# Decoder block, last two stages: routing of four batches and the small expert's second layer placed among the last causal heads

## What is computed

```python
xf = _rms(x, n2_w).reshape(-1, C)
logits = jnp.nan_to_num(xf @ gate_w.T)
probs = softmax(logits); topv, topi = top_k(probs, 2)
topv = topv / (topv.sum(-1, keepdims=True) + 1e-08)
wts = zeros((N, E)).at[arange(N)[:, None], topi].add(topv)
o0 = _gelu(xf @ e0_up.T) @ e0_down.T
o1 = silu(xf @ e1_w1.T) * (xf @ e1_w2.T) @ e1_down.T
o2 = _gelu(_gelu(_gelu(xf @ e2_l1.T) @ e2_l2.T) @ e2_l3.T) @ e2_l4.T
o3 = _gelu(_gelu(xf @ e3_down.T) @ e3_up.T) @ e3_out.T
moe = wts[:, 0:1]*o0 + wts[:, 1:2]*o1 + wts[:, 2:3]*o2 + wts[:, 3:4]*o3
return x + moe        # first 64 channels of moe are zero; a layernorm follows
```

## Time and profile before

| what | value |
|---|---|
| three runs | 1126.34, 1134.78, 1134.48 us (median 1134.48) |
| profiled execution, its own time | 1130.39 us |
| its span, first to last instruction | 1128.6 us |
| mean granted PE clock | 0.928 of full speed |

### The profile page before, as it was taken

One profiled execution on the slowest core, in us unless ns is written; L12 is line 12 of the kernel. 1 busy time (PEld: TensorE's weight loads), 2 busy tenths in 40 slices (PEclk: granted clock), 3 DMA queues, 4 the chain that ended last, 5 costly groups with the idle time before them and its releaser, 6 DMA issues.

```text
span 1128.6 us, 22127 instructions
## 1 busy us (share of the span) xinstructions
PE 971.2 (86%) x8864; PEld 702.0 (62%) x8864; DVE 679.3 (60%) x1584; ACT 587.8 (52%) x1382; POOL 289.5 (26%) x297
## 2 busy tenths in 40 slices
PE   7997879987879998999898788888888888978995
PEld 4664556665458875666566566666566666646754
DVE  3346544664949955666565577766767666649204
ACT  4632555553438865454554345555456464666441
POOL 3421332100230007111121131222122132355443
PEclk9997878979889998999998889999999899988998
DMA  9350543500769978432262333304304104000001
GB/s 308 113 91 21 128 101 73 123 12 1 237 198 325 323 255 258 156 129 90 82 192 82 87 114 110 110 29 134 97 29 138 28 1 164 6 1 1 1 1 33
DMA packets 66678, 123.71 MB, mean 110 GB/s; under 512 B 11632, under 2 KB 41968, under 8 KB 62496
## 3 DMA queue, kind: packets, MB, share of 16 engines
q1 hardware_dynamic: 64528, 117.48, 34.1%
q0 software_dynamic: 2048, 4.82, 1.4%
HBM read 86.30 MB, written 35.92 MB: 108 GB/s over the span
## 4 chain that ended last, share of the span: by engine, by line
PE 53%; DVE 24%; ACT 11%; DMA 5%; issue 4%; POOL 2%; SPq 1%; DVEq 0%; ACTq 0%; POOLq 0%
PE psum L413 36%; ACT s_p L2803 3%; DVE s_p L2845 3%; DVE s_max L2834 2%; PE psum L2762 2%; PE psum L1410 2%; PE psum L2773 2%; DVE s_pT L2826 1%; DMA raw_wd<-in_wd 1%; PE psum L568 1%; PE psum L2236 1%; DVE junk L1930 1%; DVE s_max L687 1%; PE psum L2946 1%; PE psum L2754 1%
## 5 line engine op out<-in xcount | busy, mean ns | idle before, releaser
L2803 ACT ACTIVATE s_p<-psum,s_max 112x375 f32<-112x375 f32 x128 | 72.2, 569 | 98.8 <-DVE s_max L2834 98.8
L734 POOL TENSOR_TENSOR rstd<-meanvar,minus_half 112x1 f32<-112x1 f32 x40 | 25.7, 643 | 244.7 <-DVE meanvar L679 176.0
L687 DVE TENSOR_REDUCE s_max<-psum 112x2 f32<-112x750 f32 x64 | 59.4, 935 | 36.6 <-PE psum L568 35.8
L2762 PE MATMUL psum<-ident,s_p 112*125 112x112 f32 x384 | 63.1, 298 | 7.6 <-ACT s_p L2803 3.2
L2834 DVE TENSOR_REDUCE s_max<-psum 112x1 f32<-112x375 f32 x128 | 63.7, 540 | 2.2 <-PE psum L2754 2.0
L2754 PE MATMUL psum<-s_k,s_q 64*112 64x375 f16 x384 | 47.6, 354 | 20.2 <-ACT s_p L2803 8.2
L413 PE MATMUL psum<-Wv,ctx 128*125 128x512 f16 x240 | 60.6, 404 | 3.4 <-issue 2.6
L2762 PEld LDWEIGHTS psum<-ident,s_p 112*125 112x125 f32 x384 | 51.8, 200 | 17.5 <-DVE s_max L2834 5.2
L413 PE MATMUL psum<-ctx,Wk 128*128 128x375 f16 x320 | 61.7, 328 | 0.0
L3200 POOL TENSOR_TENSOR rs<-ms,minus_half 112x32 f32<-112x32 f32 x8 | 43.5, 5438 | 69.2 <-DVE ms L3128 69.2
L628 ACT ACTIVATE s_k<-psum 128x375 f16<-128x375 f32 x64 | 31.2, 491 | 52.2 <-PE psum L413 51.8
(11 more groups left out here) (402 smaller groups left out, 2481.4 us busy)
## 6 DMA issues: line engine op xcount, KB each, us to landing
keys<-s_k SPq DMA_DIRECT2D x64, 187.5 KB, 2.3
s_k<-keys SPq DMA_DIRECT2D x8, 1500.0 KB, 7.6
values<-s_v SPq DMA_DIRECT2D x48, 224.0 KB
s_v<-values SPq DMA_DIRECT2D x16, 672.0 KB
raw_wg<-in_wg SPq DMA_DIRECT2D x8, 1024.0 KB, 6.7
raw_wu<-in_wu SPq DMA_DIRECT2D x8, 1024.0 KB, 6.9
raw_wd<-in_wd SPq DMA_DIRECT2D x8, 1024.0 KB, 7.9
s_kd<-k_halves SPq DMA_DIRECT2D x48, 93.8 KB, 3.8
```

The costliest lines, as they stand in the source:

```text
L687: VE.tensor_reduce(s1_max[b % 2][:, 2 * p:2 * p + 2], rings["s1"][unit][0:N, :, 0:S], X, ALU.max, negate=True).then_inc(*V.up("max1", n))
L2762: ins = TE.transpose(rings["t4"][unit][0:SCH, c * N:(c + 1) * N], p[:, c * SCH:(c + 1) * SCH], ident[0:N, 0:N])
L2803: SC.activation(rings["p4"][2 * n + j], rings["s4"][(n, j)][0:N, 0:S], ACT.Exp, bias=s4_max[b % 2][:, h:h + 1], accum_out=s4_sum[b % 2][:, ...
```

## The change

1. The routing's arrays move to a region of their own (`route_m`), and each step works on one half (4 batches). Half 0 is routed in the causal heads' stage: stream `s5_first_route` waits for `gate5` of batch 3, then places a copy of the router's products (`tp6`), the steps and the exponential. Half 1 is routed in the last stage. `gate5` of batches 4 and 5 wait for the copy.
2. The filler's order: `gate5` 0 to 3 first, then the 14 products with e3_down ahead of e0_up, then four units `ly5`, which are e3_up for half 0 with Gelu, copy and subtraction, and then `gate5` 4 and 5. The Gelus of `la` follow the same new order and wait for the exponential of half 0.
3. In the last stage the second layer of e3 for half 0 is gone, and the sums come by halves: experts 0 and 1 half 0, e3_up half 1, expert 3 half 0, e2_l1 half 0, experts 0 and 1 half 1, e2_l1 half 1, expert 3 half 1. The weight splits follow: e3_out now comes ahead of e2_l1.

```diff
-    AHEAD = [(name, f) for name in ("e0_up", "e3_down", "e1_w1", "e1_w2")
+    AHEAD = [(name, f) for name in ("e3_down", "e0_up", "e1_w1", "e1_w2")
...
+    step("ly5", "T ly, A gelu, A lh, G ll", "misc5", "A gelu", 1150)
+    step("tp6", "V +2, V tp6")
+    step("r6", "V r6")
+    step("r6x8", "V +3, V r6")
+    step("exp6", "A exp6")
...
     def s5_ahead():
         yield from until(("out", 4, B - 1), ("xfT5e", 3), ("split5p", FIRST[3], KC - 1))
+        for b in range(4):
+            yield [("gate5", b)]
         for i, at in enumerate(AHEAD):
             yield from until_banks(1)
             yield [("aheadV" if i % 2 else "aheadA", *at)]
-            if 4 <= i < 8:
-                yield [("gate5", i - 4)]
+        for f in range(HT):
+            yield from until(("la", "e3_down", 0, KC - 1), ("la", "e0_up", 0, f), ("split5", "e3_up"))
+            yield from until_banks(1)
+            if f == 0:
+                rings["hidden"].take(("e3_up", 0), (T, ("ax", 3, 0, 3)))
+            yield [("ly5", "e3_up", 0, f)]
         for b in (4, 5):
             yield from until(("xfT5e", b))
             yield [("gate5", b)]
 
+    def s5_first_route():
+        yield from until(("gate5", 3))
+        yield [("tp6", 0)]
+        yield from route_until_exp(0)
+        yield [("exp6", 0)]
+        yield from route_behind_exp(0)
+
+    def route_until_exp(hf):
+        for n in range(5):
+            yield [("r6", hf, n)]
+
+    def route_behind_exp(hf):
+        for n in range(5, 22):
+            place(("r6x8" if n in (8, 9) else "r6", hf, n))
+            if n % 2:
+                yield None
+
     def s5_first_gelu():
-        yield from until(("s5e", B - 1, 3))
+        yield from until(("s5e", B - 1, 3), ("exp6", 0))
...
         elif what == "gate5":
             pe.wait_ge(A["oT4", B - 1, 1])
+            if b >= 4:
+                pe.wait_ge(V["tp6", 0])
             gate_product(b, T.up("gate5", b))
...
+        elif what == "ly5":
+            name, hf, f = at
+            raw_, dst = raw_rows(name, hf, f), rings["hidden"][name, hf]
+            act.wait_ge(T["ly", *at], G["ll", "e0_up", 0, f])
+            SC.activation(raw_, ring[unit][:, 0:HALF], ACT.Gelu,
+                          scale=1 / WSCALE).then_inc(*A.up("gelu", *at))
+            act.wait_ge(A["gelu", *at])
+            SC.activation(dst[:, 0, f, :], raw_, ACT.Copy).then_inc(*A.up("lh", *at))
...
     def s6_add(e, hf):
-        yield from until(("r6", 21), ("split5", ("e0_down", "e1_down", "e2_l4", "e3_out")[e]))
+        yield from until(("r6", hf, 21), ("split5", ("e0_down", "e1_down", "e2_l4", "e3_out")[e]))
...
         yield from s6_layer("e3_down", 1)
-        yield from s6_layer("e3_up", 0)
-        for e in range(2):
-            for hf in range(2):
-                yield from s6_add(e, hf)
+        yield from s6_add(0, 0)
+        yield from s6_add(1, 0)
         yield from s6_layer("e3_up", 1)
-        for hf in range(2):
-            yield from s6_layer("e2_l1", hf)
-            yield from s6_add(3, hf)
+        yield from s6_add(3, 0)
+        yield from s6_layer("e2_l1", 0)
+        yield from s6_add(0, 1)
+        yield from s6_add(1, 1)
+        yield from s6_layer("e2_l1", 1)
+        yield from s6_add(3, 1)
...
-                (w16_w, "e2_l1", ("ly", "e3_down", 1, 1)), (w16_w, "e3_out", ("ax", 0, 0, 0)),
-                (w16_w, "e2_l2", ("ax", 0, 0, 3)), (w16_w, "e2_l3", ("ax", 0, 1, 3)),
-                (w16_w, "e2_l4", ("ax", 1, 0, 3))):
+                (w16_w, "e3_out", ("ly", "e3_down", 1, 1)), (w16_w, "e2_l1", ("ax", 0, 0, 3)),
+                (w16_w, "e2_l2", ("ax", 1, 0, 3)), (w16_w, "e2_l3", ("ax", 3, 0, 3)),
+                (w16_w, "e2_l4", ("ax", 0, 1, 3))):
```

More of the change, by code:

```diff
@@ L2734, in build @@
           follow(s5_out, range(1, B, 2)),
-          s5_first_weights(), s5_first_gelu(), filler=ahead_units)
+          s5_first_weights(), s5_first_route(), s5_first_gelu(), filler=ahead_units)
     for units in ahead_units:
-        for unit in units:
+        for unit in units or ():
             place(unit)
@@ L3026, in gpsimd_gelu_low, with take_logits, scalar_route @@
                          ALU.subtract).then_inc(*G.up("ll", name, hf, f))
+    def take_logits(hf):
+        here = slice(4 * hf, 4 * hf + 4)
+        VE.tensor_copy(tp5[:, here], psum[0:N, GATE_BANK, 4 * hf * E1:(4 * hf + 4) * E1].rearrange(
+            "p (b e) -> p b e", e=E1)).then_inc(*V.up("tp6", hf))
+    def scalar_route(hf):
+        here = slice(4 * hf, 4 * hf + 4)
+        act.wait_ge(V["r6", hf, 4])
+        SC.activation(tp5[:, here], lg5[:, here], ACT.Exp).then_inc(*A.up("exp6", hf))
@@ new lines, in vector_route @@
+    def vector_route(what, hf, n):
+        if n:
+            dve.wait_ge(A["exp6", hf] if n == 5 else V["r6", hf, n - 1])
+        else:
+            dve.wait_ge(V["tp6", hf])
+        if what == "r6":
+            route(hf, n).then_inc(*V.up("r6", hf, n))
+            return
+        for b in range(4 * hf, 4 * hf + 4):
+            ins = VE.max(top5[:, b, :], pr5[:, b, :]) if n == 8 else \
+                VE.max_index(top5_i[:, b, :], top5[:, b, :], pr5[:, b, :])
+            ins.then_inc(*(V.up("r6", hf, n) if b % 4 == 3 else V.up()))
@@ new lines, in route, with wide4 @@
+    def route(hf, n):
+        here = slice(4 * hf, 4 * hf + 4)
+        mx, den, ts = (sm5[:, i, here] for i in range(3))
+        ok5_, tp5_, lg5_, cl5_, wt5_, pr5_, top5_ = (
+            t[:, here] for t in (ok5, tp5, lg5, cl5, wt5, pr5, top5))
+        def wide4(t):
+            return t.unsqueeze(2).to_broadcast([N, 4, E1])
+        if n == 0:
+            return VE.tensor_tensor(ok5_, tp5_, tp5_, ALU.is_equal)
+        if n == 1:
+            return VE.tensor_scalar(lg5_, tp5_, FMAX, -FMAX, ALU.min, ALU.max)
+        if n == 2:
+            return VE.copy_predicated(cl5_, ok5_, lg5_)
+        if n == 3:
+            return VE.tensor_reduce(mx, cl5_, X, ALU.max)
+        if n == 4:
+            return VE.tensor_tensor(lg5_, cl5_, wide4(mx), ALU.subtract)
+        if n == 5:
+            return VE.tensor_reduce(den, tp5_, X, ALU.add)
+        if n == 6:
+            return VE.reciprocal(den, den)
+        if n == 7:
+            return VE.tensor_tensor(pr5_[:, :, 0:E1], tp5_, wide4(den), ALU.mult)
+        if n == 10:
+            return VE.tensor_tensor(ts, top5_[:, :, 0], top5_[:, :, 1], ALU.add)
+        if n == 11:
+            return VE.tensor_scalar(ts, ts, 1e-8, WSCALE, ALU.add, ALU.mult)
+        if n == 12:
+            return VE.reciprocal(ts, ts)
+        if n == 21:
+            return VE.tensor_tensor(wt5_, wt5_, tp5_, ALU.add)
+        k, m = divmod(n - 13, 4)
+        dst = (wt5_, tp5_)[k]
+        if m == 0:
+            return VE.tensor_copy(ek5[:, k, here], top5_i[:, here, k])
+        if m == 1:
+            return VE.tensor_tensor(dst, iota8[:, 0:E1].unsqueeze(1).to_broadcast([N, 4, E1]),
+                                    wide4(ek5[:, k, here]), ALU.is_equal)
+        if m == 2:
+            return VE.tensor_tensor(sm5[:, 3, here], top5_[:, :, k], ts, ALU.mult)
+        return VE.tensor_tensor(dst, dst, wide4(sm5[:, 3, here]), ALU.mult)
@@ L3213, in gpsimd_s5 @@
                              ALU.subtract).then_inc(*G.up("xf16", b))
-        elif what == "la":
+        elif what in ("la", "ly5"):
             gpsimd_gelu_low(*at)
@@ L3309, in s6_route @@
     def s6_route():
-        yield [("gate6",)]
-        for n in range(5):
-            yield [("r6", n)]
-        yield from until(("exp6",))
-        for n in range(5, 22):
-            place(("r6x8" if n in (8, 9) else "r6", n))
-            if n % 2:
-                yield None
+        yield [("gate6", 1)]
+        yield from route_until_exp(1)
+        yield from until(("exp6", 1))
+        yield from route_behind_exp(1)
     def s6_split():
@@ L3394, in scalar_s6 @@
             elif what == "exp6":
-                act.wait_ge(V["r6", 4])
-                SC.activation(tp5[:], lg5[:], ACT.Exp).then_inc(*A.up("exp6"))
+                scalar_route(*at)
             elif what == "ly":
@@ L3416, in vector_s6 @@
         fence(dve, 5)
-        mx, den, ts = sm5[:, 0, :], sm5[:, 1, :], sm5[:, 2, :]
         def vector_gated_high(hf, f, raw_):
```

116 lines of the change are left out of this document (42 added, 74 removed).

## The result

The changed kernel takes 1145.95 us (median of 20 runs, 1134.08 to 1155.07), the kernel before 1129.52 us (20 runs, 1116.24 to 1138.74). The ratio is 1.0148, with a 95% interval of 1.0120 to 1.0177: slower by 1.5%, clear of the noise, and outside the range that was given (1123 to 1139 us).

What follows compares the result with a forecast made beforehand. It took PE's wait for DVE's first add of sums as the bound: +4.3 +0.3 −3.8 = +0.8 us on 1130.39 makes 1131.2, plus 1.1 for the runs' mean gives 1132.3 us, range 1123 to 1139.

Steps and rivals of the forecast that it cites:

- What bounds the end: Last stage: the end is fixed by when PE may pass its wait for DVE's first add of sums.
- Part 3: Last stage, from its first matmul to the first add: less routing and fewer POOL subtractions bring the add 3.8 us sooner.
- The clock behind the wait: Last stage: the clock's dip around the wait costs 2.3 us before and after; change 0, bounds −1.4 and +1.
- Part 1: Before the last stage: four early second-layer products load ACT ahead of the last batch's squares; stage starts 4.3 us later.
- Part 2: Causal heads: early routing of batches 0 to 3, about 6 us on DVE, mostly covered; +0.3 us, bounds −0.7 and +3.
- A: Rival, chance 0.22: ACT's idle time before the last stage hides the moved layer, stage only 1.5 us later; 1129 us.
- B: Rival, chance 0.08: in the last stage the wait and both clock dips vanish, products fill idle time; −12.7, 1119.8 us.
- D: Rival, chance 0.10: in the last stage second-half routing stays slow, first add 1.5 us sooner instead of 3.8; 1134.6 us.
- C: Rival, chance 0.13: in the heads early routing collides with POOL's power and delays the maxima, +6.4 us; 1138 us.
- the routing's short operations: Sign of being right: in the causal heads, routing operations of 0.2 us on DVE around 960 us.
- the wait for the first add: Sign of being right: in the last stage PE still waits near 5 us, ending near 1036.5 us.
- the 312 matmuls behind it: Sign of being right: after PE's wait in the last stage, 312 matmuls run unbroken before the second deep layer.

Runs made afterwards that it cites:

- e0_up: Not a run: the code's name for expert 0's early products, which the change places behind the small expert's first layer; no time of its own.
- e3_other_rows: Changed kernel, with the early second layer's Gelu writing into rows read long before; 1146.41 us beside 1134.19 for the kernel before, ratio 1.0082.
- e2_layer_only: Kernel before, with only the small expert's second layer of half 0 moved early and its first layer ahead of expert 0; 1134.14 us beside 1134.19, ratio 1.0009.
- e6: Changed kernel with gate products spread and the second layer of half 0 back in the last stage; ratio to the kernel before 0.9944, run again 0.9996.
- e4: Changed kernel with the four gate products spread behind the fifth to eighth early product; 1130.42 us beside 1134.19 for the kernel before, ratio 0.9970.
- e5: Changed kernel, gate products still first, routing of half 0 held back until the eighth early product; 1144.36 us beside 1133.71 before, ratio 1.0027.
- e1_route_only: Changed kernel with the small expert's second layer of half 0 back in the last stage; 1142.31 us beside 1134.19 before, ratio 1.0013.
- e11_gates_first_only: Kernel before, with only the four gate products put together ahead of the 14 early products; 1134.02 us beside 1132.00, ratio 1.0037.
- e8: Changed kernel with the four gate products together behind the first two early products; 1135.38 us beside 1133.71 for the kernel before, ratio 1.0000.
- e12: The changed kernel itself, run once more without any edit; 1146.02 us beside 1131.72 for the kernel before, ratio 1.0114.

## Why the prediction was wrong, step by step

- **What bounds the end: right.** The moment of the first add decides, the 588 matmuls behind it are unbroken in both, 79.77 and 79.22 us.
- **Part 3, −3.8 us: right in mechanism and nearly in size.** S to wait fell by 4.7 us, inside the bounds. POOL's subtractions went from ten to six, and routing steps beside them were slow, one or two behind them fast:

```profile
1045.93 6.00 POOL L3077 TENSOR_TENSOR hidden<-raw,hidden 128x448 f16<-128x448 f32 x6
```

```profile
1048.02 0.97 DVE L3131 TENSOR_SCALAR sm<-sm 112x4 f32<-112x4 f32 x1
...
1049.23 0.74 DVE L3139 CAST ek<-top_i 112x4 f32<-112x4 uint32 x1
...
1052.19 0.17 DVE L3139 CAST ek<-top_i 112x4 f32<-112x4 uint32 x1
```

- **The clock behind the wait: wrong, small.** I held its dip equal. The 48 matmuls behind the wait take 7.04 us where 48 at full clock take 4.12, so the dip costs 2.9 us against 2.3: part of the +0.5 from wait to l2.
- **Part 1, +4.3 us: wrong in this kernel, right alone.** The failed step is "Working through the written order with its costs: the 14 early products are used up at the same place as before". They are not: with the gates in front they are used up sooner (13 of them lie in the heads in place of 11), so the four new products meet the `la` units one by one, and each Gelu waits for POOL. I priced that wait at 0.5 us once and 0.1 us once; it came in every round. e3_other_rows puts it at 4.5 us, and e2_layer_only, where the old order holds, shows 4.3 us to the squares and 4.5 at S.
- **Part 2, +0.3 us: wrong, the main error.** The failed step is the bound "−0.7 (four gate products of at most 0.47 us go first in place of two of 1.18 us, so the last batch starts a little sooner)". The routing, on which I spent the argument, costs nothing that can be seen where the gates are spread (e6: out to S 54.5 us, before 54.9; it then runs later, at 982 to 999 us). The order of the fillers, which I had taken for a small gain, costs 12.1 us of the 15.3 (e4: out to S 58.1 in place of 70.2). Of the 6.3 us in the heads, up to 1.7 are the clock's dip at the gates (6.8 of 10.9 in the repetition), and the other 4.6 two early products more (1.2 to 1.3 us each) and 1.8 us of idle time, most of it in the pair of heads without products between its steps (with the routing held back, in e5, a product stands there and PE waits 1.8 us in place of 0.9 and 2.4). "The clock. ... Change 0" fails here too: I had looked at S and at the wait alone, not into the heads. Where the gates stand in front, the routing adds nothing that can be seen without the clock: the heads less the clock's part take 43.3 us in e1_route_only and 44.0 in e11_gates_first_only, which has no early routing. The 5.1 us of clock between them are e1's dip behind the hole, and whether the routing has a part in that is open.
- **The rivals.** A (tail hides the layer), B and D did not occur. C had the right sign and the wrong mechanism: POOL didn't slow the early routing: its power starts at 976.64 us in the changed kernel, and the last two steps beside it take 0.17 us each. What I had no rival for is the order of cheap fillers.
- **The forecast itself.** The changed order's gain of 4.7 us in the last stage is real, and out to S takes back three times as much. Of the signs that I gave, the routing's short operations, the wait for the first add (4.22 us, forecast near 5) and the 312 matmuls behind it came; the last stage's first matmul stood at 1026.32 us, forecast near 1008 (7 us of this are the later "out").

## What to carry to other kernels

A filler is there to cover waits of PE. The short gate products did that badly when they stood together, and the granted clock dipped in each profile in which they did: put such products one at a time between wide ones rather than all in front, even if something else would like to start early. When a change reorders the fillers, walk the whole placed order again from the first to the last of them, since every unit behind it moves. And where a buffer is used again, look at what stands between its last reader and the new writer in the placed order, not at whether the reader is "long done" in the old trace.

## What the runs showed of the hardware

- In all eight profiles with the four gate products together, the granted clock dipped to 0.50 or 0.51 (1.2 GHz, the lower of the two levels) somewhere in the heads, by windows of 2 us; in the six with the products spread it never did. Seven of the eight dip while the gate products run or within 3 us behind them, e8 for over 13 us. How busy PE was doesn't separate them: the clock fell in e11 0.41 us after the first gate product had begun, behind 5 us with 3.47 us of work, and it stayed at 1.00 in the kernel before at the same distance from "out", also behind 3.47 of 5 us. What differs up to the fall is which product those last 0.4 us hold, a gate product or an early one; e5 and e1 fell at the same place, e4 stayed like the kernel before. In e8 PE's row was busy for 12.8 us on end, and the clock stayed at 0.50 all the while. Why the clock falls in the one order and not in the other no run shows. The page "TensorE: Matmul & The Clock Gate" of the Trainium skill (section Part 1: The HAM clock gate) ties the clock to how busy PE has been recently. Read by the busy column of the profile, that rule would treat e11 and the kernel before alike; the trace doesn't agree with such a reading, and the measurement decides.
- Where the dips fall differs from run to run. One program (changed, e12) had them at the gates alone, and at the gates and behind the hole; e3, with the same placed order, behind the hole alone. Its heads took 46.5, 51.1 and 47.0 us. Kernels without dips repeat to a tenth of a microsecond. The same page and section call the moment of the switch variable from run to run, and there the trace agrees: one placed order, three different sets of dips.
- Beside POOL's subtractions not only two-input operations on DVE were slow, as I had read from the earlier trace rows, but also a scalar operation on 112x4 (0.97 us, 0.17 among the heads) and a cast (0.74, 0.17 there).
